# A four-layer attention and ffn kernel on one core: score tiles in 32-row strips, stages that overlap at their ends, and a quantised ffn in place

## What is computed

```
x = x + xattn0(ln(x), ctx)         # 16 heads of 8, softmax over 512 keys, biases on q, k, v, o
x = x + ffn0(ln(x))                # quantised: W_in per column, W_out per row to 8 bit,
                                   # the tokens and the hidden values to 16 bit with ONE scale
                                   # for all of them: round(v * 32767 / max|v|); gelu between
x = x + xattn1(ln(x), ctx)
x = x + moe1(ln(x))                # 8 experts of 512, top 2 of 8 by a gate, one shared expert
x = x + xattn2(ln(x), ctx, mask)   # mask over 256 queries x 512 keys
x = x + block2(ln(x))              # an inner layer norm, causal self-attention with 16 heads
                                   # of 8 over 256 keys, then 8 experts of 256 with silu(a)*b
x = x + xattn3(ln(x), ctx, mask)   # mask over keys; scale 1/sqrt(128)
x = x + moe3(ln(x))                # 8 experts of 512, top 2, layer norm of the sum
```

## Time and profile before

| | |
|---|---|
| time, median of 3 runs | 2367.53 us (2366.49 to 2370.65) |
| profiled execution, span from first to last instruction | 2364.8 us |
| instructions | 46942 |
| PE, PE weight loads, DVE, ACT, POOL busy | 90%, 59%, 53%, 55%, 21% |
| mean granted clock of TensorE | 0.932 |
| DMA | 117.5 MB, 50 GB/s |

### The profile page before, as it was taken

One profiled execution on the slowest core, in us unless ns is written; L12 is line 12 of the kernel. 1 busy time (PEld: TensorE's weight loads), 2 busy tenths in 40 slices (PEclk: granted clock), 3 DMA queues, 4 the chain that ended last, 5 costly groups with the idle time before them and its releaser, 6 DMA issues. The chain is left out here.

```text
span 2364.8 us, 46942 instructions
## 1 busy us (share of the span) xinstructions
PE 2118.7 (90%) x14264; PEld 1391.1 (59%) x14264; DVE 1247.3 (53%) x3806; ACT 1289.5 (55%) x2226; POOL 499.4 (21%) x1107
## 2 busy tenths in 40 slices
PE   2999975699997999979999978887997999989998
PEld 1555543355555889844554545555885555548887
DVE  5667646566662222256666544444564667642343
ACT  0777752377774444346666644444331787864443
POOL 4221210111211222121111111222232222212221
PEclk9999987699998999979999978788997899999999
DMA  3322310622310000052213011110003423300000
GB/s 81 90 80 54 94 29 0 169 71 64 89 40 10 1 0 0 1 143 67 69 45 85 28 41 42 54 54 10 0 0 101 119 72 76 89 1 1 4 4 10
DMA packets 101314, 117.53 MB, mean 50 GB/s; under 512 B 12710, under 2 KB 68412, under 8 KB 101180
## 3 DMA queue, kind: packets, MB, share of 16 engines
q1 hardware_dynamic: 101180, 115.94, 18.5%
HBM read 70.82 MB, written 45.09 MB: 49 GB/s over the span
## 5 line engine op out<-in xcount | busy, mean ns | idle before, releaser
L929 PE MATMUL ps_s<-kst,qz 96*128 96x512 f32 (+2 forms) x1280 | 601.2, 485 | 60.6 <-DMA qz<-q_parts 40.4
L758 ACT ACTIVATE prob<-ps_t 128x512 f32<-128x512 f32 (+1 forms) x896 | 492.3, 581 | 265.7 <-PE ps_t L941 109.9
L941 PE MATMUL ps_t<-qz,kst 128*128 128x512 f32 (+1 forms) x1152 | 464.5, 407 | 0.5 <-ACT prob L758 0.2
L1313 DVE CUSTOM_DVE_ANT_0 junk<-ps_s,mask_q 128x512 bf16<-128x512 f32 x512 | 342.1, 688 | 167.1 <-PE ps_s L929 160.4
L1304 DVE TENSOR_REDUCE mx<-ps_s 128x1 f32<-128x512 f32 x512 | 334.5, 684 | 138.5 <-PE ps_s L929 137.3
L929 PEld LDWEIGHTS ps_s<-kst,qz 96*128 96x128 f32 x1280 | 256.4, 205 | 237.1 <-DVE mx L1313 59.9
L961 PE MATMUL ps_av<-prob,vaug 128*32 128x256 f32 (+1 forms) x4608 | 363.5, 390 | 3.4 <-ACT avs L794 3.1
L1160 PEld LDWEIGHTS ps_s<-w_ffn,prob 128*128 128x128 f32 x2688 | 315.4, 192 | 8.7
L1160 PE MATMUL ps_s<-w_ffn,prob 128*128 128x128 f32 x2688 | 319.2, 276 | 0.0
L798 ACT ACTIVATE qz<-ps_m 32x1024 fp32r<-32x1024 bf16 x160 | 162.7, 1017 | 152.6 <-PE ps_m L971 149.0
L941 PEld LDWEIGHTS ps_t<-qz,kst 128*128 128x128 f32 x1152 | 225.0, 197 | 33.7 <-issue 9.8
(11 more groups left out here) (200 smaller groups left out, 2403.3 us busy)
## 6 DMA issues: line engine op xcount, KB each, us to landing
kst<-k_parts SPq DMA_DIRECT2D x32, 768.0 KB, 6.1
k_parts<-k_hi SPq DMA_DIRECT2D x64, 256.0 KB, 2.9
qz<-q_parts SPq DMA_DIRECT2D x160, 96.0 KB
q_parts<-q_hi SPq DMA_DIRECT2D x80, 128.0 KB, 2.4
ctxT<-in_ctxT SPq DMA_DIRECT2D x32, 256.0 KB, 4.7
k_parts<-k_lo SPq DMA_DIRECT2D x32, 256.0 KB, 2.9
q_parts<-q_lo SPq DMA_DIRECT2D x40, 128.0 KB, 2.4
w_ffn<-in_F_w SPq DMA_DIRECT2D x18, 256.0 KB, 3.9
```

Of the source, the lines that this page charges most:

```text
L758: nc.scalar.activation(dst, src, ACT.Exp, bias=bias).then_inc(sig["exp_done"], 1)
L929: pe.matmul(ps_s[TURN[i]][:, 0:nk], qz[p][0:96, g, j, q * 128:(q + 1) * 128], kst[p][0:96, g, 0:nk], start=True, stop=True).then_inc(sig[" ...
L941: mm = pe.matmul(dst, kst[p][:, g, kt * 128:(kt + 1) * 128], qz[p][:, g, 2 * half:2 * half + 2, q0:], start=True, stop=mask in (None, "keys"))
L1313: dve.tensor_tensor_reduce(junk[:, TURN[i], 0:nk], src, m, 1.0, -3.0e38, ALU.add, ALU.max, mx[:, buf, i:i + 1])\
```

## The change

Nearly every function is touched. What it does, part by part:

- **Strips.** A head's operand takes one strip of 32 rows: 8 fixed rows (rows of ones and zeros, three rows for the maxima, and for A3 the key mask, halved, in two rows) and 24 rows of parts. `qz` with its zeros becomes `qst`, without. `scores` takes strip j of `qst` and `kst`; `scores_T` takes strip j of `kst` and of `qmx`, a copy of the queries' group with the maxima added, made by one fp32r and two bf16 matmuls and one 256-column copy on ACT. A step of the loop issues two scores of 512 columns in strips 0 and 1 (or 2 and 3), then four transposed products of 256 columns in the two other strips, in two banks. The product with the values follows for two key tiles at once, at every second step. For A2 and AS the mask's matmul opens the bank, before the others.
- **Who does what.** Normalising, the high part of K and Q, the inner normalisation and adding the output bias go to POOL; the copy of the values goes to ACT; the output bias, with the values' bias folded in, is made once a stage and added to x in advance. DVE takes the negative maximum. In A3 neither DVE nor ACT handles the mask.
- **Ahead.** K, Q and the strips of a batch are made two batches ahead instead of one, loaded per group. A2 runs on into AS without a break.
- **Ends.** The last batch of A1, AS and A3 makes the first weights and the first tokens of the ffn behind it; the attention's last output steps stand between the ffn's first products. The last block of F1 and F2 carries K, Q, V, the bias and 16 (14) score tiles of the next attention (`LEADS`).
- **F0.** `rounded` has two passes; the hidden values are rounded where they lie, in halves of a block; `xfT` has two buffers; the last maximum is taken in quarters; the output's bias is added to x in advance, on POOL; `add` is one operation.
- **Start.** The load of x is split, the first block comes early with the weights of K; quantising W_in goes over PE's transposes instead of an all-reduce on POOL.
- **Loops.** All loops are written out; waits are for constants.

```diff
@@ constants
-ROWS = 3 * DH
+STRIP = 32
+FIXED = 8
+K_ROWS = (FIXED, FIXED + 2 * DH, FIXED + DH)
+Q_ROWS = (FIXED, FIXED + DH, FIXED + 2 * DH)
...
+HEAD_S = [0, 1, 2, 3, 0, 1, 2, 3]
+HEAD_T = [2, 3, 0, 1, 2, 3, 0, 1]
+NEXT_FFN = {"A1": "F1", "AS": "F2", "A3": "F3"}
+LEADS = {
+    "F1": {(0, "mid"): "K0", (0, "end"): "XT0", (1, "mid"): "Q0", (1, "end"): "V0", (2, "mid"): "B0", (2, "end"): "B1",
+           (3, "mid"): "K1", (3, "end"): "XT1", (4, "mid"): "Q1", (4, "end"): 0, (5, "mid"): 1, (5, "end"): 2,
+           (6, "mid"): 3, (6, "end"): 4, (7, "mid"): 5, (7, "end"): 6, (8, "mid"): "MT", (8, "end"): 7},
...
@@ sync: how strips come back
+                for g in range(NG):
+                    sp.dma_start(kst[p][:, g, 0:nk].bitcast(F32), scratch["k"][p][128 * g:128 * (g + 1), 0:nk]).then_inc(stacked[p][g], 16)
+                    sp.dma_start(qst[p][:, g, :].bitcast(F32), scratch["q"][p][128 * g:128 * (g + 1), :]).then_inc(stacked[p][g], 16)
@@ scalar
-                nc.scalar.activation(qz[bt.parity][96:128, g, :, :], ps_mb[96:128, :].rearrange("p (j s) -> p j s", j=HG),
-                                     ACT.Copy).then_inc(sig["mt_read"], 1)
+                nc.scalar.activation(qmx[:, g % 2, :], ps_m[:, 0:S], ACT.Copy).then_inc(sig["mt_read"], 1)
@@ tensor: scores
-                pe.matmul(ps_s[TURN[i]][:, 0:nk], qz[p][0:96, g, j, q * 128:(q + 1) * 128], kst[p][0:96, g, 0:nk],
+                pe.matmul(dst, qst[p][strip, g, q * 128:(q + 1) * 128], kst[p][strip, g, 0:nk],
                           start=True, stop=True).then_inc(sig["s_ready"], 1)
@@ tensor: scores_T
-                mm = pe.matmul(dst, kst[p][:, g, kt * 128:(kt + 1) * 128], qz[p][:, g, 2 * half:2 * half + 2, q0:],
-                               start=True, stop=mask in (None, "keys"))
+                mm = pe.matmul(dst, kst[p][strip, g, kt * 128:(kt + 1) * 128], qmx[strip, g % 2, seen(ph, kt):],
+                               start=not opened, stop=not opened or c == 1)
@@ tensor: a step of the loop
+                                if half == 0:
+                                    for n in range(2):
+                                        if ATT[ph]["mask"] in ('full', 'causal') and unit_at(ph, k, n) is not None:
+                                            opening_mask(ph, bt, g, unit_at(ph, k, n))
+                                    for n in (2 * k, 2 * k + 1):
+                                        if ahead[0]:
+                                            scores(*ahead, n)
+                                    for c in range(2):
+                                        for n in range(2):
+                                            if unit_at(ph, k, n) is not None:
+                                                scores_T(ph, bt, g, unit_at(ph, k, n), c)
+                                if half == 1 and past[0] and (k, ATT[past[0]]["nk"]) in ((1, SK), (1, S), (3, SK)):
+                                    for kt in (k - 1, k):
+                                        values(*past, kt)
@@ tensor: behind the last batch
+                        wait(pe, "fxt_read", cnt.at("fxt_read", nph, 0))
+                        first_product(nph, 0, 0)
+                        misc("AVT0", ph, end)
+                        misc("AVT1", ph, end)
+                        first_product(nph, 0, 1)
+                        misc("ONT", ph, end)
+                        gate_product(nph, 0)
+                        second_product(nph, 0, 0, 0)
+                        misc("O", ph, end)
@@ vector: maximum, rounded, F0
-                    dve.tensor_reduce(mx[:, buf, i:i + 1], src, AX.X, ALU.max).then_inc(sig["max_done"], 1)
+                    dve.tensor_reduce(mx[:, buf, i:i + 1], src, AX.X, ALU.max, negate=True).then_inc(sig["max_done"], 1)
...
-                link(dve.tensor_scalar(dst, src, scale, -A16 - 1.0, ALU.mult, ALU.max))
-                link(dve.tensor_scalar(dst, dst, A16, ROUND, ALU.min, ALU.add))
-                return dve.tensor_scalar(dst, dst, ROUND, None, ALU.subtract)
+                link(dve.tensor_scalar(dst, src, scale, ROUND, ALU.mult, ALU.add))
+                return dve.tensor_scalar(dst, dst, ROUND, A16, ALU.subtract, ALU.min)
...
+                def quantise_h(blk, half):
+                    h = hid[:, :, 512 * blk + 256 * half:512 * blk + 256 * (half + 1)]
+                    rounded(h, h, svec[:, 4:5]).then_inc(sig["hq_done"], 1)
...
+                    dve.scalar_tensor_tensor(out=dst, in0=ps_s[blk % 2][:, :].rearrange("p (q d) -> p q d", q=TB), scalar=svec[:, 5:6],
+                                             in1=dst, op0=ALU.mult, op1=ALU.add).then_inc(sig["x_new"], 1)
@@ gpsimd: F0's bias
+                for blk in range(NBLK):
+                    dst = x_tok[:, TB * blk:TB * (blk + 1), :]
+                    pool.tensor_tensor(dst, dst, boutb[:, :].rearrange("p (o d) -> p o d", o=1).to_broadcast([128, TB, D]), ALU.add).then_inc(x_biased, 1)
```

More of the change, by code:

```diff
@@ L1109, in output @@
+                        if c == 1 and blk + 1 < NBLK:
+                            turn_block(ph, blk + 1)
+                turn_block(ph, 0)
+                for blk in range(NBLK):
+                    hidden(blk)
+                def output(blk, half):
+                    p = blk % 2
+                    wait(pe, "hq_done", cnt.at("hq_done", ph, blk, half))
                     wait(pe, "x_new", cnt.at("x_new", ph, blk) - 2)
-                    for q in range(TB):
+                    for q in (2 * half, 2 * half + 1):
@@ L1179, in body @@
                             mm.then_inc(sig["ct_ready"], 1)
-                        second_product(blk, e, e)
+                        if blk or e:
+                            second_product(ph, blk, e, e)
+                        if last and ph in LEADS:
+                            lead({"F1": "A2", "F2": "A3"}[ph], LEADS[ph].get((e, "end")))
                         if e == 4 and not last:
@@ L1371, in attention @@
+            def attention(ph):
+                b0 = Batch(0)
+                if ph in LED:
+                    for pair in range(LED_PAIRS[ph], 8):
+                        lead(ph, pair)
+                elif ph != "AS":
+                    wait(dve, "x_new", cnt.start("x_new", ph))
+                    wait(dve, "rstd_done", cnt.start("rstd_done", ph))
                 if ph == "A0":
                     quantise_weights()
-                if ph != "AS":
-                    lay_v(ph, b0)
@@ L1400, in attention @@
+                                what = slots(ph).get((g, k, half))
+                                if what in ("AVT0", "AVT1", "O") and pph:
+                                    misc(what, pph, pbt)
+                batches(body)
+                if ph == "A2":
+                    return
+                end = Batch(B - 1)
                 if ph == "A0":
                     convert_rest()
-                for what in ("AVT0", "AVT1", "O"):
+                for step in range(3, 6):
+                    result_statistics(ph, end + -1, step)
@@ L1481, in experts @@
+                add(0)
+                new_statistics(0)
+                for half in range(2):
+                    quantise_h(2, half)
+                add(1)
+                for half in range(2):
+                    quantise_h(3, half)
+                add(2)
+                new_statistics(1)
+                add(3)
+                new_statistics(2)
+                new_statistics(3)
             def experts(ph):
                 ne = 9 if ph == "F1" else 8
-                src_of = y_tok if ph == "F2" else x_tok
```

1406 lines of the change are left out of this document (824 added, 582 removed).

## The result

The changed kernel takes **1893.7 us** (median of 3 runs, 1877.2 to 1895.2) where the kernel before takes 2367.5: ratio 0.798, 95% interval 0.793 to 0.803. Run again later, beside the experiments, it had a median of 1876.9 us (5 runs, 1872.6 to 1898.5), ratio 0.794 (0.790 to 0.797). Medians and ranges leave out two single executions in a slower state of the chip, 1901.9 us of this kernel and 1868.0 us of the kernel of experiment 5. The forecast was 1848. The profiled execution discussed here has a span of 1891.9 us.

What follows compares the result with a forecast made beforehand. PE was taken to set the time in attention (except AS) and expert ffns, the rest being handovers. Terms -220 -80 -70 -47 -39 -22 -20 -22 = -520 took the span from 2364.8 to 1845, so 1848 us; range 1700 to 2050.

Steps and rivals of the forecast that it cites:

- The forecast of a step: Attention loops: six strip matmuls side by side take 0.25 us plus 0.09 for tile shape; 16 x 0.35 = 5.6 us a batch.
- three engines colliding: A0, A1, A3: PE, DVE and ACT at 22.5 to 22.8 us can't all run full; 2.7 us added, 25.5 a batch.
- (a): Attention and ffns: nothing collides, batches of 23, 29.5 and 19.5 us, ffns 10 us better; 1734 us in all; 17%.
- (c): Attention steps: row strips don't overlap at all, 1.04 us a step, batch 33.9; 2188 us in all; 4%.
- (b): Attention steps: six weight loads stand in a row, 0.76 us a step, batch 29.5; 2032 us in all; 12%.
- (d): Attention loops: the clock behaves as in AS, 0.82, batch 28 us; +60, 1908 us in all; 10%.
- (f): Attention: granted clock stays at 1.2 GHz while strips run, PE's batch 45 us; slower than before, 2674 us; 4%.
- (e): Handovers stay, as PE blocks on a lead whose POOL or DMA step is late; +80, 1928 us; 8%.
- the last two groups: A0, A1, A3 loops: 3 us less than 8 x 25.5, as the last two groups have no scores ahead of them.
- The leads: Next attention's work in F1's and F2's last blocks: 10 us of lead for F1, 13 for F2's tail and lead.
- The loops written out: Expert ffns: F1 at 61 us a block, 244 for 256.7; loops give 6 us in F2 and 8 in F3.
- What would show it: Signs: strips' scores start together, A0 batch 24 to 27 us, PE 80 to 90% there, PE gaps under 3 us except F0's.

Runs made afterwards that it cites:

- experiment 5: Changed kernel with, in A0, A1 and A3, DVE's maxima over half the columns and each tile's second transposed-score matmul left out: 1841.3 us (unaltered 1876.9).
- experiment 2: Changed kernel with the transposed scores put in the same two 32-row strips as the step's scores: 1967.6 us (unaltered 1876.9).
- the second execution: The changed kernel, unaltered, profiled again: span 1875 us, where the first profiled execution had 1892.
- experiment 1: Changed kernel without the unused all-reduce on POOL in A0's first batch: 1863.5 us (unaltered 1876.9).
- experiment 9: Changed kernel with one more ACT table switch (Exp) per block of the expert ffns and blocks 1 to 3 of F0: 1887.0 us (unaltered 1876.9).
- experiment 4: Changed kernel with each tile's second transposed-score matmul left out in A0, A1 and A3, ACT reading the first half twice: 1871.7 us (unaltered 1876.9).

## Why the prediction was nearly right, and where not

**Right in size.** Faster by about a fifth: 474 us gained, 520 forecast. The batch of A0 came out 0.4 us above the 25.5 forecast, A2 1.1 below 32.5, AS at 20.4 to 20.7 at full clock where I took 22. That AS as a whole met its forecast, 177.7 us for 176, is luck: the stretch at the lower clock made up for the shorter batches, and without it AS took 159.4 us from result to result, for 180.0 here. The start, 40.8 for 41, was met too, but no run took its parts apart. The forecast of a step was 0.35 us where it is 0.44 at its shortest: **the pair of scores was mis-sized**. I took 0.25 for two strips side by side because column strips of the value product are that quick, and 0.09 for the change of shape behind them; they take 0.43 with that change, against 0.57 for two full-height ones (185.11 to 185.68). Sixteen steps are 7.0 us where I had 5.6; the rest of PE's batch is 15.1 where I had 16.9, so that PE's own work, 22.1 us, came out near my 22.5 by two errors against each other. The 2.7 us for three engines colliding was the least argued term. The steps take 3.9 us more than sixteen of the shortest, so the size was too small, and my picture of it (DVE's store of scores) is not shown: DVE with 8 us less gave back 0.5. The same count gives the batch before 19.2 us in steps where I had 15.0 from the spacings alone, and 16.3 outside them where I had 20.4, so the saving outside the steps is 1.2 us and not 3.5.

**Rivals.** (a), nothing collides and 23 us a batch, falls by 25.9. (c), no overlap of strips, falls by the step of 0.44 and by experiment 2. (b), loads in a row at 0.76 a step, falls by 0.44. (d), the clock of AS in the other attentions, did not come: A0, A1 and A3 had 0.98, 0.97 and 0.97. AS had 0.84 in the profile above, but in the second execution the 44 us at 1.2 GHz are missing. (f) did not come: one stretch of AS stood at 1.2 GHz, no attention loop as a whole did. (e) falls, by PE gaps of at most 3.5 us around F1, F2 and F3.

A step here is 1.04/0.44 = 2.4 times as quick as before. The Trainium skill (TensorE: Matmul & The Clock Gate, Part 3) has 3.07 times for four strips of 512 columns each. By it the matmuls of a step took 0.31 us in the prediction; with the 0.09 for the change of shape that makes 0.40, an estimate, nearer to the 0.44 than my 0.35. A step here has four strips with 512 columns each, but in two of them as two matmuls of 256, so its figure is neither confirmed nor refuted.

**The terms that failed**, in order of size:
- A0 +19: 10 of it is the unused all-reduce, which the diff shows and my account of POOL left out. I counted its normalising, splitting and bias, and never asked what this call costs, though the trace of the kernel before has it, with 6.17 and 6.69 us of idle time around it.
- A0, A1, A3, each: 8 x 0.4 = 3 us of batch, and **3 us for the last two groups**, which were to be shorter and aren't: the loop of experiment 1 takes 210.1 us for eight batches, 26.3 each, more than the steady 25.9. Where those last 3 us go was not looked into.
- The leads. 10 us were put down for F1's; its last block takes 74.4 in experiment 1 (743.2 to 817.6) against 61.5 for the one before, so 13; in the profile above 78.7, with the clock at 0.92. F2's lead and tail were to cost 13; the lead alone costs 12.6. All the same it pays: without it A3 starts 18 us later.
- The loops written out. Their share of F1, F2 and F3 was never taken back alone; experiment 9 only rules out the table loads there.
- F0 came out better by 5. Its parts, taken singly: the pass 5.4 (2.5 forecast, as the second half's supply was not thought of), the table loads some 3 (3.8), the bias 2.1 (up to 5, four adds of 1.3).

**What would show it** was right for the strips' starts, the batch between 24 and 27 us, A0 and A1's clock, and wrong elsewhere: PE was to be at 80 to 90% in A0 and stands at 98 in a batch (92 over the loop with its stall), ACT was to be above 85% and is at 83, and A2's PE was to be above 95% and is at 94 (29.46 of 31.4). The gap before A3 is 3.5 us, not under 3. Busy time in rows of small overlapping matmuls counts waits as work; the share told me nothing either way.

## What to carry to other kernels

Before an engine is called the bound, take work from it and see; a busy share of 98% stood over 3.9 us of waiting in 26, and neither of the two obvious engines was alone in the way. When small matmuls are spread over row strips, price the widest pair in the step: the others may ride free. On POOL look at the idle time around an all-reduce (here 5.6 us ahead of it, 6.9 behind), not at its own 0.4 us, and keep POOL's long two-input adds away from DVE's passes. When an experiment puts something back, count it in the trace: experiment 9 put back twice what had been taken out.

## What the runs showed that I had not expected

- Around an all-reduce POOL stands idle 5.5 to 6.2 us ahead and 6.7 to 7.5 behind, where nothing else holds it up, with or without an earlier call.
- DVE's pass over 128x512 took 0.49 us alone and 1.58 beside an add on POOL.
- The clock fell to 0.50 for 44 us in the middle of AS, with PE 93% busy right before, in one execution and not in the next.
- Leaving out 32 matmuls a batch (experiment 4) made a step 0.01 us shorter.
